# A hybrid eight-layer kernel on one core: the layer norms that stand between stages get their factor from one matmul with ones, and ln and exp over the whole chunk

## The reference, cut to what matters

```python
def _layernorm(x, axis=-1, eps=1e-05):
    m = jnp.mean(x, axis=axis, keepdims=True)
    v = jnp.var(x, axis=axis, keepdims=True)
    return (x - m) / jnp.sqrt(v + eps)

x = L0_attn_a_x                                     # 2048 tokens of 128 channels, float32
x = x + _L0_attn_a_ref(_layernorm(x), ...)          # gated linear attention        L_GLA
x = x + _L0_ffn_ref(_layernorm(x), ...)             # ternary FFN                   L_FFN0
x = x + _L0_attn_b_ref(_layernorm(x), ...)          # state space layer             L_SSM
x = x + _L0_ffn_ref(_layernorm(x), ...)             # the same FFN                  L_FFN1
x = x + _L1_attn_a_ref(_layernorm(x), ...)          # top-k attention               L_TOPK
x = x + _L1_ffn_ref(_layernorm(x), ...)             # int8 FFN                      L_INT0
x = x + _L1_attn_b_ref(_layernorm(x), ...)          # linear attention, 16 heads    L_LIN
x = x + _L1_ffn_ref(_layernorm(x), ...)             # the int8 FFN again            L_INT1
```

## Time and profile before

| | |
|---|---|
| median of 3 runs | 1245.7 us (1245.2 to 1250.65) |
| the profiled execution | 1257.61 us, of which the span of the trace is 1255.8 us |
| PE, DVE, ACT, POOL busy | 83%, 66%, 58%, 40% of the span |
| granted TensorE clock, mean of the span | 0.834 of full |
| standing layer norms | 7 to 31, 194 to 203, 303 to 313 and 343 to 355 us of the span |

### The profile page before, as it was taken

The page is one execution under the profiler, slowest core; times in us unless marked ns, Lnnn a source line. Parts: engine busy times, 40 slices in busy tenths (PEclk is TensorE's granted clock), DMA queues, the critical chain, the costliest instruction groups (busy, mean ns, idle before and its releaser), DMA issues. The chain is left out here.

```text
span 1255.8 us, 20275 instructions
## 1 busy us (share of the span) xinstructions
PE 1046.1 (83%) x6856; PEld 749.3 (60%) x6856; DVE 827.2 (66%) x1788; ACT 733.0 (58%) x1842; POOL 502.0 (40%) x508
## 2 busy tenths in 40 slices
PE   6669988999789997488788978899889877887786
PEld 2268875766257653356665657667666765665444
DVE  2367656454354548798998799989798886222146
ACT  2853235775077865378477757877676756534245
POOL 2000000000000005777777777777777777760000
PEclk7679889998579997598689778889899778768579
DMA  7000001000000004824531343322333332310000
GB/s 226 20 1 2 1 2 38 1 1 1 0 1 1 1 1 106 206 59 94 131 68 47 77 104 65 68 58 50 65 68 68 67 67 60 79 35 1 1 1 34
DMA packets 74489, 61.99 MB, mean 49 GB/s; under 512 B 31570, under 2 KB 59028, under 8 KB 73876
## 3 DMA queue, kind: packets, MB, share of 16 engines
q1 hardware_dynamic: 58516, 36.31, 12.7%
q0 software_dynamic: 15872, 24.41, 8.7%
HBM read 52.53 MB, written 8.13 MB: 48 GB/s over the span
## 5 line engine op out<-in xcount | busy, mean ns | idle before, releaser
L657 POOL DMA_INDIRECT gathered_rows<-key_table,idx_T x496 | 494.1, 996 | 596.6 <-DMA key_table<-key_rows 445.3
L994 PE MATMUL bank<-ident,rotated_rows 128*96 128x128 f32 x512 | 94.1, 315 | 4.7 <-DVE rotated_rows L2022 4.7
L672 PE MATMUL bank<-index_k_hi,index_q 128*128 128x512 f32 (+5 forms) x160 | 79.7, 500 | 21.9 <-ACT index_relu L1489 12.1
L2022 DVE TENSOR_TENSOR rotated_rows<-gathered_rows,rank_rope 128x384 f32<-128x384 f32 x128 | 70.9, 554 | 39.3 <-DMA gathered_rows<-key_table,idx_T 38.8
L1517 ACT ACTIVATE probs<-probs,attn_columns 128x208 f32<-128x208 f32 x128 | 59.5, 465 | 63.6 <-DVE attn_columns L2040 62.2
L1506 ACT ACTIVATE turned_rows<-bank 96x512 f32<-96x512 f32 x128 | 74.5, 582 | 31.7 <-PE bank L994 31.3
L1990 DVE SCALAR_TENSOR_TENSOR index_sums<-index_relu,iw,index_sums 128x512 f32<-128x512 f32 (+5 forms) x120 | 77.7, 648 | 18.8 <-ACT index_relu L1489 14.4
L1489 ACT ACTIVATE index_relu<-bank 128x512 f32<-128x512 f32 (+5 forms) x160 | 76.8, 497 | 22.2 <-PE bank L672 20.9
L1999 DVE MAX8 top<-index_sums 128x8 f32<-128x96 f32 (+15 forms) x64 | 78.2, 1222 | 1.2
L1018 PE MATMUL bank<-ident,probs 128*128 128x128 f32 x128 | 43.4, 339 | 42.6 <-ACT probs L1517 42.2
L2001 DVE FIND_INDEX8 idx_u<-top,index_sums 128x8 uint32<-128x96 f32 (+15 forms) x64 | 78.1, 1220 | 0.0
(11 more groups left out here) (281 smaller groups left out, 2567.5 us busy)
## 6 DMA issues: line engine op xcount, KB each, us to landing
gathered_rows<-key_table,idx_T POOLq DMA_INDIRECT x496, 2.7
q_window_in<-q_l SPq DMA_DIRECT2D x64, 64.0 KB
q_picked_in<-q_g SPq DMA_DIRECT2D x64, 64.0 KB
h<-in_h SPq DMA_DIRECT2D x2, 1024.0 KB, 8.0
q_l<-rotated SPq DMA_DIRECT2D x8, 256.0 KB
q_g<-rotated SPq DMA_DIRECT2D x8, 256.0 KB
q_lat<-q_latent_sb SPq DMA_DIRECT2D x8, 256.0 KB, 3.8
q_window_in<-q_lat SPq DMA_DIRECT2D x16, 128.0 KB
```

Of the source, the lines that this page charges most:

```text
L657: pool.indirect_dma_start(out=G[b][:, q, :], out_offset=None, in_=key_table[0:index_width(i), :], in_offset=bass.IndirectOffsetOnAxis(ap=i ...
L672: return pe.matmul(out_, lhsT, rhs, start=start, stop=stop, **kw)
L994: last = pe.transpose(bank[2][0:ROW, j * P:(j + 1) * P], GR[n % 2][:, j, :], ident[:])
L2022: v.tensor_tensor(GR[n % 2], G[i % 2][:, 4 * g:4 * g + 4, :], rank_rope[:].unsqueeze(1).to_broadcast([P, 4, ROW]), ALU.mult).then_inc(a_ro ...
```

## The change

In the five standing layer norms ACT squares the centred chunk straight into `xn`. PE multiplies the square by `ones`, all 128 x 512 of it, so that the sum of squares of each token stands on all partitions in bank 6+u. ACT takes Ln (scale 1/128, bias eps) of that bank into `xn`, and then Exp with scale -0.5 in place: the factor. DVE multiplies bank 4+u by it, into `xn`. The copy, the four small matmuls, the Sqrt, the reciprocal, the diagonal and the spreading matmul are gone there. The woven layer norms keep the old way; since `ln_diag` and `ln_inv` are now counted by those alone, their counts get new numbers (`spread_index`, `LNS`).

The product now reads bank 4+u until it is applied. So `merge_weights`, which writes bank 4, does the eight `Muv` products first and waits for the first chunk of the pair to be applied before the eight `Mq` products.

```diff
-        LNT = 4 * L_INT0
+        LNT, LNS = 4 * L_INT0, 10
+        SPREADS = [(L_FFN0, 1), (L_SSM, 0), (L_FFN1, 1), (L_TOPK, 0), (L_TOPK, 1)]
+        def spread_index(k, r):
+            return 18 + 2 * r if k == L_INT1 else 2 * SPREADS.index((k, r))
...
 (PE)
             def ln_spread(k, r):
                 for u in range(2):
-                    pe.wait_ge(ln_diag, 4 * k + r * 2 + u + 1)
+                    pe.wait_ge(ln_diag, spread_index(k, r) + u + 1)
                     mm(bank[6 + u], ones[:], inv_diag[:, u, :]).then_inc(ln_inv, 1)
             def layer_norm(k, pairs=(0, 1)):
                 for r in pairs:
                     ln_center(k, r)
-                    ln_mean(k, r)
-                    ln_spread(k, r)
+                    for u in range(2):
+                        pe.wait_ge(ln_squared, 4 * k + r * 2 + u + 1)
+                        mm(bank[6 + u], ones[:], chunk(xn, 2 * r + u)).then_inc(ln_var, 1)
...
             def merge_weights():
                 pe.wait_ge(t_w, 64)
                 for h in range(NH):
+                    mm(bank[2 + h // 4][0:DC, (h % 4) * P:(h % 4 + 1) * P], WuvT[:, h, :], Wout[:, h, :])
+                pe.wait_ge(ln_applied, LN0 + 4 * L_SSM + 3)
+                for h in range(NH):
                     last = mm(bank[4][0:DCQ, h * DC:(h + 1) * DC], WuqT[:, h, :], WukT[:, h, :])
-                for h in range(NH):
-                    last = mm(bank[2 + h // 4][0:DC, (h % 4) * P:(h % 4 + 1) * P], WuvT[:, h, :], Wout[:, h, :])
                 last.then_inc(t_wm, 1)
...
 (ACT)
             def layer_norm(k, pairs=(0, 1)):
                 for r in pairs:
-                    ln_square(k, r)
-                    ln_sqrt(k, r)
+                    for u in range(2):
+                        act.wait_ge(ln_centered, 4 * k + r * 2 + u + 1)
+                        fn(chunk(xn, 2 * r + u), bank[4 + u], ACT.Square).then_inc(ln_squared, 1)
+                    for u in range(2):
+                        act.wait_ge(ln_var, 4 * k + r * 2 + u + 1)
+                        own = chunk(xn, 2 * r + u)
+                        steps.did(fn(own, bank[6 + u], ACT.Ln, scale=1.0 / P, bias=eps_col))
+                        fn(own, own, ACT.Exp, scale=-0.5).then_inc(ln_sd, 1)
+                steps.leave(steps.k, 1)
...
 (DVE)
             def layer_norm(k, pairs=(0, 1)):
                 for r in pairs:
-                    ln_invert(k, r)
-                    ln_apply(k, r)
-                steps.leave(steps.k, 1)
+                    for u in range(2):
+                        dve.wait_ge(ln_sd, 4 * k + r * 2 + u + 1)
+                        own = chunk(xn, 2 * r + u)
+                        v.tensor_tensor(own, bank[4 + u], own, ALU.mult).then_inc(ln_applied, 1)
```

More of the change, by code:

```diff
@@ L1112, in tail_step @@
                 elif name == "spread":
-                    pe.wait_ge(ln_diag, LNT + L + 1)
+                    pe.wait_ge(ln_diag, LNS + L + 1)
                     mm(o_, ones[:], i_diag).then_inc(ln_inv, 1)
@@ L1583, in tail_step @@
                     if L >= 1:
-                        act.wait_ge(ln_diag, LNT + L)
+                        act.wait_ge(ln_diag, LNS + L)
                     steps.did(fn(i_sd, o_[:, 0:C // P], ACT.Ln, bias=eps_col))
@@ L1721, in ln_apply @@
                     c = 2 * r + u
-                    dve.wait_ge(ln_inv, 4 * k + c + 1)
+                    dve.wait_ge(ln_inv, spread_index(k, r) + u + 1)
                     v.tensor_tensor(xn[:, c * C:(c + 1) * C], xn[:, c * C:(c + 1) * C], bank[6 + u], ALU.mult)\
@@ L1933, in queries_rotate @@
                 if c == 0 and half == 0:
-                    dve.wait_ge(ln_inv, 4 * L_TOPK + 4)
+                    dve.wait_ge(ln_inv, spread_index(L_TOPK, 1) + 2)
                 if c >= 1 and b == 0:
@@ L2081, in tail_step @@
                     else:
-                        dve.wait_ge(ln_inv, LNT + L)
+                        dve.wait_ge(ln_inv, LNS + L)
                     v.tensor_tensor(i_diag.rearrange("p (j t) -> p j t", t=P),
@@ L2086, in tail_step @@
                 elif name == "spread":
-                    dve.wait_ge(ln_inv, LNT + L + 1)
+                    dve.wait_ge(ln_inv, LNS + L + 1)
                     v.tensor_tensor(xn[:, tokens], xn[:, tokens], o_, ALU.mult).then_inc(ln_applied, 1)
```

## The result

| | before | after |
|---|---|---|
| median of 20 runs each | 1250.93 us (1241.08 to 1260.62) | 1260.59 us (1253.0 to 1268.3) |
| the profiled execution | 1257.61 us, span 1255.8 | 1256.71 us, span 1254.9 |

The ratio is 1.0093, with a 95% interval of 1.0069 to 1.0118. The changed kernel is slower, and by more than 0.5%. Yet the two traces say the opposite: the span of after is 0.9 us shorter. So one trace of each can't explain the result, and the first question was which of them was not typical. More runs than stood behind the table ahead also moved the median of before, from 1245.7 to 1250.93.

The account below looks back on a forecast made before the run. At the norms no engine is full; the chain from the second Square to the second product counts. Terms -1.85 + 3.5 - 4.4 + 1.05 = -1.7 us gave 1244.0 us, range 1238 to 1250.

Parts of the forecast that it names:

- Loads: ACT in the standing norms: a table load ahead of every Ln and Exp, four a pair at 1.30 us each.
- Rival (a): Standing norms: the compiler keeps one table set for Ln and Exp, sparing three loads a pair; -19.4 us, 1226 us; chance 0.03.
- The length of a pair: Each standing norm: 8.6 us from the end of the second Square to the end of the second product.
- L_GLA, -1.85: Gated attention: ACT's low-rank copy runs 0.8 us sooner and a later table load goes, gaining about 1.05 us.
- L_FFN0, +3.5: First ffn: the pair takes 8.6 us instead of 5.88, +2.7, and starting at the low clock costs 0.85.
- L_SSM, -4.4: State space layer: merges run beneath ACT's chain, DVE becomes last, first scan at 315.35 us instead of 319.78.
- L_FFN1, +1.05: Second ffn: the pair takes 8.6 us instead of 7.55, at a clock that was low already.
- The clock: PE: quiet for some 8 us ahead of L_FFN0, which then starts at the low clock, costing 0.85 us.
- Rival (c): Clock stays high through L_SSM's merges into its loop and L_FFN0 loses nothing to it: 1239 to 1241 us; chance 0.07.
- Rival (b): Both ffn stages begin at the low clock and stay there; 12 us longer costs 3.6, 1247.6 us; chance 0.12.
- Sum: Whole kernel: four stage terms give -1.7 us on the profiled execution, and the same was taken off the median: 1244.0 us.

Follow-up runs that it names:

- e3: The changed kernel with one request for a table set having both Ln and Exp at the start of each standing norm: 1228.09 us, 0.9819 of before.
- e1: The kernel before, run again without any edit, as a second trace: 0.9981 of before.
- e6: The kernel before with the new norm only in the pairs of L_FFN0 and L_FFN1, and the new merge order: 1.0076 of before.
- e10: e6 with one request for the table set having both Ln and Exp at the start of its two new norms: 0.9969 of before.
- e7: The changed kernel with unread matmuls added behind the ones matmuls in the pairs of L_GLA, L_FFN0 and L_FFN1: 1.0033 of before.
- e9: The kernel before with only three more table loads ahead of the Sqrt, two in L_FFN0 and one in L_FFN1: 1260.21 us, 1.0077 of before.

## Why the prediction was wrong, step by step

Forecast -1.7 us and 1244.0, range 1238 to 1250; measured +9.7 us and 1260.6. Of the 16.6 us between, 5.2 are the median of before, which I took from three runs and which moved by that much with twenty. The other 11.4 are the change.

- **Loads.** Right: two sets, a load ahead of every Ln and Exp, 1.30 us from its start to the next start, the first beneath the matmuls. Rival (a) fell by the trace, and e3 shows that its price was near. The rule of the Trainium skill, "ScalarE: Activation LUTs", section "Table sets: the hidden batching unit", that ln and exp share a set is true of the set that e3 asks for by name, and not of the one that is taken for a Ln by itself.
- **The length of a pair.** Right, 8.6 us in four pairs and 8.96 in the first of L_GLA. The terms as written add up to 8.5; the Exp took 0.63 and not 0.60. The reason given for the short old pair of L_FFN0, that no load stands in it, doesn't hold alone: the second pair of L_GLA has no load either and took 8.25, by the two long products of VectorE, which the prediction passed over.
- **L_GLA, -1.85.** The tile loop began at 72.8, 72.3 and 72.7 us, against 72.7 in the trace that I had worked from: the gain was 0. The Square of the last chunk came at 22.84, not 21.9, since the first pair was longer and PE's centring ran at the low clock (2.05 us for one chunk); and behind the load that went, the next activation waited for logits at that clock. Against the mean of the four traces of before, 70.7, this part is a loss of 1.9, and against the mean of the eight with the old norm there, 69.5, a loss of 3.1. I had held the new chain against an old pair of 8.25 us, which in other runs takes 4.3.
- **L_FFN0, +3.5.** To the Silu +3.4 against the same trace, and +4.3 against the mean of four, 19.7. The 0.9 us that the stage lost behind its Silu were not in the sum.
- **L_SSM, -4.4.** From the first Square to the first scan -4.1 against the same trace, but -2.2 against the mean of four; and over the whole stretch from the Silu, with the 0.9 us of the ffn stage and 0.4 in the loop, -0.9. This is the largest error of a term. The 5.49 us for which the scan waited were real in that run, but 3.4 of them were a low clock beneath norm and merges, which isn't there in every run (2.11 in e1).
- **L_FFN1, +1.05.** Against the same trace +1.6, against the mean +2.1.
- **The clock.** Rival (c), a clock that holds, came in one half: the merges of L_SSM ran at the full level (1.93 and 1.11 us, granted clock 1.00 from 302 to 316 us), but DVE was last there and L_FFN0 did lose. Rival (b) is the nearest to what happened, at 0.12. Its clock is real: it cost 1.7 and 1.0 us behind the two ffn pairs, of which the sum had 0.85. But that is less than the 3.6 us of its upper case. What no rival had is that the old kernel has the stalls of the first trace only in some of its traces, and the changed one has its long chain of loads in all.

Against the four traces the parts add up to +1.9 - 0.2 (tile loop) + 4.3 - 0.9 + 2.1 = +7.2 us (7.1 before rounding) at the pick, and +1.4 in the means of the top-k stage, 8.5 in all, where the interval of the ratio has +8.6 to +14.8. e6 puts most of the loss into the ffn pairs, e10 and e3 show that the loads in the path cause it, and e7 shows the clock's share in L_FFN0. How the remaining us are shared between the scatter of the top-k stage and of the front isn't settled: three and four traces are too few.

The step that failed is the one from the trace to the median, under **Sum**: a profiled execution 12 us above the median of its runs was taken as if all of that lay elsewhere. I wrote that "none of that lies in a stretch that the change touches", and no row stood behind this. Up to 11.5 us of it lay in the front (478.3 against 466.8). With it failed the two terms that were gains: L_SSM at -4.4 measured -0.9 and L_GLA at -1.85 measured +1.9, both against the mean, since each was held against a stall that only some runs have.

## What to carry to other kernels

Ask for a table set with both functions ahead of an Ln and Exp that alternate, and put the request where ACT is idle: here this alone took the change from 1.0093 to 0.9819 of before. Where a longer chain leaves TensorE quiet right ahead of dense matmuls, add the low clock to the price (here 1.7 us behind 8.17 us of quiet), and look whether other work of TensorE stands between, as in e9, where it cost nothing. When a single trace stands well off the median of its runs, take a second one before a term is read from a stall in it, above all a stall on PE or an instruction that takes three times as long as the same one elsewhere in the trace.

## What the runs showed of the hardware

- The same program has fronts that differ by 11.5 us in four traces. In L_GLA most of it goes with a product of VectorE that takes 0.69 us or 2.2 us, the latter where GpSimd rounds weights at the same time; from the Sqrt to the pick it is the granted clock, with merges of 5.5 or 3.0 us in L_SSM.
- The three traces of the changed kernel agree within 0.8 us at the pick.
- A table load took 1.28 us and 1.30 us to the next start, and a program that asks for no set got one for every Ln and every Exp: 20 for ten pairs of them.
- Three such loads in the old kernel cost 9.1 us by the medians, of which the trace shows 3.4 over the longest of before, from the Sqrt to the pick. 16 matmuls of 128x512 that nobody reads brought the ratio to 1.0033 from 1.0073 to 1.0093, with intervals that overlap.
- The granted clock over the 8 us behind the first matmul of L_FFN0 was 0.65 behind 8.17 us of quiet on PE, 0.79 behind 3.24 (e10), and 1.00 behind 1.47 (before) or behind 3.03 that followed 5.3 us of added work (e7). The Trainium skill, "TensorE: Matmul & The Clock Gate", section "What's actually happening", has the array throttled by default until activity releases it; the traces agree.
